# Softmax row sums: matmuls read both key halves of the exponentials, and VectorE's addition of the halves is left out

## The reference

```python
x = x * s1[:, None, :]
x = (x - mu) * jax.lax.rsqrt(var + EPS_IN)
q = heads(jnp.einsum('bsh,oh->bso', x, q_weight) * q_dc[:, None, :])
k = heads(jnp.einsum('bsh,oh->bso', x, k_weight) * k_dc[:, None, :])
v = heads(v_flat)
attn = jnp.einsum('bhqd,bhkd->bhqk', q, k) * scale
attn = jax.nn.softmax(attn, axis=-1)
out = jnp.einsum('bhqk,bhkd->bhqd', attn, v).transpose(0, 2, 1, 3).reshape(B, S, H)
out = jnp.einsum('bsh,oh->bso', out, w_weight) * w_dc[:, None, :]
```

## Time and profile before

| what | value |
|---|---|
| timed runs, median (lowest to highest) | 718.82 us (718.27 to 719.84) |
| profiled execution, span from the first to the last instruction | 718.9 us |
| mean granted TensorE clock, share of full speed | 0.903 |
| attention stage in the profiled execution | about 0 to 300 us |
| TensorE busy | 515.4 us, 72% |
| VectorE busy | 500.2 us, 70% |
| ScalarE busy | 263.7 us, 37% |

### The profile page before, as it was taken

One profiled execution on the slowest core, in us unless ns is written; L12 is line 12 of the kernel. 1 busy time (PEld: TensorE's weight loads), 2 busy tenths in 40 slices (PEclk: granted clock), 3 DMA queues, 4 the chain that ended last, 5 costly groups with the idle time before them and its releaser, 6 DMA issues.

```text
span 718.9 us, 10868 instructions
## 1 busy us (share of the span) xinstructions
PE 515.4 (72%) x3248; PEld 302.7 (42%) x3264; DVE 500.2 (70%) x820; ACT 263.7 (37%) x513; POOL 129.9 (18%) x136
## 2 busy tenths in 40 slices
PE   3667888888888878999972100187677668888878
PEld 2555556465564634688862000011111113333357
DVE  2834858667595775467666897188898878888832
ACT  2314453445545433366673555012112112222211
POOL 5302012020120200240000246011221112222100
PEclk9868999999999998999995555589999989999999
DMA  9635161624606240040000234644454446556341
GB/s 356 216 71 103 31 129 26 113 52 80 118 16 130 51 81 1 1 175 0 0 0 1 88 117 157 77 90 86 98 98 93 92 85 128 117 115 135 84 147 51
DMA packets 44889, 64.88 MB, mean 90 GB/s; under 512 B 19536, under 2 KB 34256, under 8 KB 41152
## 3 DMA queue, kind: packets, MB, share of 16 engines
q1 hardware_dynamic: 41520, 59.26, 37.0%
q0 software_dynamic: 784, 3.15, 1.1%
q10 hardware_dynamic: 2560, 2.16, 0.9%
HBM read 41.88 MB, written 22.61 MB: 90 GB/s over the span
## 4 chain that ended last, share of the span: by engine, by line
PE 37%; issue 20%; DVE 19%; DMA 10%; ACT 7%; POOL 4%; SPq 2%; ACTq 0%; DVEq 0%; POOLq 0%
DVE zst L1378 15%; PE bank L718 6%; PE bank L965 6%; ACT ex L540 5%; PE bank L975 5%; PE bank L736 4%; DMA bst<-bd_d 3%; DMA qst<-mT 3%; PE bank L746 3%; PE bank L1061 2%; PE bank L773 2%; PE bank L727 2%; PE bank L756 2%; POOL xpart L416 2%; DVE mx L1175 2%
## 5 line engine op out<-in xcount | busy, mean ns | idle before, releaser
L1378 DVE CUSTOM_DVE_ANT_0 zst<-zst,bank,hi 128x512 f32<-128x512 f32 x256 | 191.3, 747 | 43.6 <-PE bank L965 22.2
L965 PE MATMUL bank<-xst,bst 128*128 128x512 bf16 x240 | 87.5, 404 | 102.5 <-DMA bst<-bd_d 57.7
L648 ACT ACTIVATE yb<-bank,ybias 128x512 f32<-128x512 f32 x64 | 44.1, 689 | 186.9 <-PE bank L975 182.4
L965 PEld LDWEIGHTS bank<-xst,bst 128*128 128x128 bf16 x256 | 24.7, 98 | 187.3 <-DVE zst L1378 120.5
L1175 DVE TENSOR_REDUCE mx<-bank 128x2 f32<-128x512 f32 x128 | 80.0, 686 | 18.1 <-PE bank L736 17.0
L540 ACT ACTIVATE ex<-bank 128x512 f32<-128x512 f32 x128 | 66.1, 609 | 41.1 <-PE bank L746 23.5
L975 PE MATMUL bank<-zst,cst 128*32 128x512 f32 x512 | 70.2, 621 | 0.9 <-DVE zst L1378 0.9
L1193 DVE TENSOR_TENSOR esum<-ex 128x1024 f32<-128x1024 f32 x32 | 39.1, 1223 | 42.7 <-ACT ex L540 42.7
L1237 DVE SCALAR_TENSOR_TENSOR acc<-xrp,wcv,acc 128x256 f32<-128x256 f32 x96 | 40.1, 481 | 29.4 <-ACT acc L580 28.8
L877 PE MATMUL bank<-xres,win 128*128 (+1 forms) x256 | 57.6, 382 | 1.2 <-ACT gateT L585 0.7
L718 PE MATMUL bank<-xnT,w 128*128 128x256 f32 x192 | 52.3, 422 | 5.1 <-ACT xnT L487 5.1
(11 more groups left out here) (169 smaller groups left out, 712.3 us busy)
## 6 DMA issues: line engine op xcount, KB each, us to landing
qk_d<-part SPq DMA_DIRECT2D x64, 96.0 KB, 2.5
xs_d<-xpart SPq DMA_DIRECT2D x16, 384.0 KB, 2.6
xst<-xs_d SPq DMA_DIRECT2D x32, 192.0 KB
xst<-xs_d SPq DMA_DIRECT2D x32, 128.0 KB
y_d<-yb SPq DMA_DIRECT2D x128, 32.0 KB
ytk<-y_d SPq DMA_DIRECT2D x16, 256.0 KB, 3.6
bst<-bd_d SPq DMA_DIRECT2D x32, 102.0 KB
qst<-qk_d SPq DMA_DIRECT2D x8, 384.0 KB, 4.6
```

The lines of the kernel that those rows point to most:

```text
L648: nc.scalar.activation(yb[:, par, g, :], bank[4 + n % 2][:, :], ACT.Identity, bias=ybias[:, bass.ds(i * (2 * CH // 4) + n, 1)]).then_inc(s ...
L965: mm(bank[k][:, :], bst[:, par, step, :], xst[:, par, step, :], start=True, stop=True)\
L1378: v._custom_dve(bass.dve_ops.TENSOR_ADD_SAT, out=zst[:, t % ZR, :], in0=zst[:, (t - 1) % ZR, :], in1=bank[t % 4][:, :], s0=hi[:, t:t + 1], ...
```

## The change

The tensor esum, its semaphore es_ready and VectorE's add_tiles are taken out. The sums matmuls read ex directly, once for each key half, and accumulate in PSUM: eight matmuls in a group where there were four. pv_done is set by the last of them.

```diff
-        esum = sb0("esum", [P, 2, 4, S])
...
                 if sums:
-                    pe.wait_ge(s["es_ready"], b * 4 + (g + 1))
-                    for r in range(4):
-                        ins = mm(bank[2 * o + 1][32 * r:32 * r + 32, 0:S], half_ones[:, par, :], esum[:, g % 2, r, :],
-                                 start=par == 0, stop=par == 1, skip_group_check=True)
+                    for t in range(HALVES):
+                        for r in range(4):
+                            ins = mm(bank[2 * o + 1][32 * r:32 * r + 32, 0:S], half_ones[:, par, :],
+                                     ex[:, g % 2, r, t * S:(t + 1) * S], start=par == 0 and t == 0,
+                                     stop=par == 1 and t == HALVES - 1, skip_group_check=True)
                     ins.then_inc(s["pv_done"], 1)
                     return
...
-                def add_tiles(g):
-                    dve.wait_ge(s["exp_done"], b * NH + (4 * g + 4))
-                    if not (first and g < 2):
-                        dve.wait_ge(s["pv_done"], b * 4 + (g - 1))
-                    v.tensor_tensor(esum[:, g % 2, :, :], ex[:, g % 2, :, 0:S], ex[:, g % 2, :, S:], ALU.add)\
-                        .then_inc(s["es_ready"], 1)
-
...
-                add_tiles(0)
-                add_tiles(1)
                 if more:
                     normalise(b + 2, False)
-                add_tiles(2)
                 attend(0)
-                add_tiles(3)
                 if not last:
                     dve.wait_ge(s["mt_done"], b + 1)
                     maxima(b + 1, 0, EARLY)
```

More of the change, by code:

```diff
@@ L218, in build @@
             cast1 part_ready pw ld_q0 ld_q1 ld_k0 ld_k1 m_row smax_done maxes mt_done mT_ready st_done exp_done
-            es_ready pv_done att_ready wu_done x1_ready wcomp wgain pconst xr_done xr_in tap3_ready gate_done
+            pv_done att_ready wu_done x1_ready wcomp wgain pconst xr_done xr_in tap3_ready gate_done
             gate_out conv_done xcT_ready xcT_used raw_ready tok_ready tok_taken xn_ready sq_done part0 part1 rem0
```

## The result

| | median us | lowest to highest | runs |
|---|---|---|---|
| before | 719.33 | 718.27 to 720.86 | 4 |
| changed | 727.29 | 726.17 to 730.94 | 4 |

The ratio is 1.0135, 95% interval 1.0092 to 1.0178: the changed kernel is slower by 8 us by the medians and by 9.7 us by the ratio (0.0135 x 719). All medians in this document are over every execution, while the ratios leave out three slow ones: 720.24 us of e8, 1704.4 us of e9, and 774.79 us of the kernel before beside e9 to e11.

What follows compares the result with a forecast made beforehand. The prediction took a chain of waits, not a busy engine, to bound the kernel. Six seams 7.7, the seventh 0.9 and the last sample 0.8 us gave +9.4, so 718.8 became 728.2 us, range 725.0 to 731.0.

Steps and rivals of the forecast that it cites:

- The unit, 0.43 us: Attention sums on TensorE: each group doubled from four to eight matmuls takes 0.43 us longer, 1.07 against 0.64.
- Rival 1: Sums matmuls: weight loads of added rounds not hidden, each exposed group costs 0.64 us, total 732.8 us; chance 0.04.
- Three of four groups exposed in six seams: Ends of samples 0 to 5: sums groups 0, 1 and 3 each add 0.43 us, 1.29 a seam, 7.7 in all.
- Rival 2: Six seams: group 3 hidden because transposes already wait for something else, 2.6 us less, 725.6 us; chance 0.09.
- The seventh seam, +0.86: Seam without transposes: last sums end before the maxima, so only groups 0 and 1 count, +0.86 us.
- 1.5 us either way: Seventh seam: TensorE's clock drop may fall earlier or later, or miss L773, changing the time by up to 1.5 us.
- The last sample, +0.78: Last sample: exponentials 0.86 us later, sums directly behind L763 end at 292.90 against 292.12, +0.78 us.
- rival 3: Sums doubling free in TensorE's idle time; only the last sample changes, -0.5 us, 718.3 us; chance 0.05.
- buys less than 0.1 us: Last sample: removing both adds on the chain gains under 0.1 us, as the exponentials were only just ahead.
- rival 4: Seams: VectorE is the hidden bound, so removing the adds makes the kernel faster, -1.7 us, 717.1 us; chance 0.04.
- The sum: Whole kernel: six seams 7.7, seventh seam 0.9 and last sample 0.8 us give +9.4 us.
- the same for this purpose: Whole kernel before: profiled span 718.9 us and median of timed runs 718.82 us taken as equal.

Runs made afterwards that it cites:

- e8: Changed kernel, sums of groups 0 and 1 directly behind their weighting, next sample's transposes ahead of group 3's sums: 714.5 us, ratio 0.9948.
- e9: Kernel before, additions kept, with only the next sample's transposes moved ahead of the sums of group 3: 720.41 us, ratio 1.0014.
- e11: Repeat of e8, the changed kernel with sums directly behind their weighting and transposes first: 715.33 us, ratio 0.9952.
- e3: Changed kernel with eight sums matmuls for groups 0 and 1, four for groups 2 and 3: 723.86 us, ratio 1.0059.
- e4: Changed kernel with eight sums matmuls for group 3 alone, four for the others: 722.53 us, ratio 1.0037.
- e5: Changed kernel with eight sums matmuls for group 2 alone, four for the others: 718.58 us, ratio 0.9985.
- e2: Changed kernel with four sums matmuls in every group, no additions, second key half left out: 717.44 us, ratio 0.9979.
- e1: Kernel before with VectorE's additions kept and the sums matmuls doubled, both rounds reading esum: 727.85 us, ratio 1.0114.
- e7: Changed kernel with the sums of groups 0 and 1 moved ahead of the next scores, directly behind their weighting: 717.58 us, ratio 0.998.

## Why the prediction was right

**The unit, 0.43 us.** Right: 1.04 against 0.61 us on the chain, 512 records with a mean of 383 ns. The nearest row, L763, had given the price exactly. Rival 1, open weight loads, is out: 16 loads of 32 columns take 0.59 us beside 1.07 us of matmuls in the timeline of the changed kernel, and the group is 0.43 us longer, not 0.64. The rule of the Trainium skill ("TensorE: Matmul & The Clock Gate", Part 3) that loads overlap matmuls in flight only with another row group doesn't describe these column strips, where all loads have all 128 rows; the measurement decides.

**Three of four groups exposed in six seams.** Right: 1.25 to 1.28 us a period against 1.29 forecast, and e3, e4 and e5 give 0.83, 0.40 and 0. Rival 2 is out by e4.

**The seventh seam, +0.86.** The mechanism was right and a part of it came back. From the second set of scores (249.35 before, 254.44 after) to the score behind attT (268.04 and 273.99) it takes 18.69 us before and 19.55 after, exactly 0.86 more. From there to the transposes of the maxima it takes 8.47 us and then 7.97: TensorE's clock fell later. Before, the granted clock is 0.50 from 268 us to 274 us. The windows of the changed kernel answer to the earlier trace rows:

```profile
271.00:274.00 3.00, 0.41 (x4) 0.13 (x4) 2.96 (x5) 0.00 (x0) 0.00 (x0) 1.00 0.00 0
274.00:277.00 3.00, 2.18 (x11) 0.60 (x12) 3.00 (x6) 0.00 (x0) 0.00 (x0) 0.86 0.00 0
277.00:280.00 3.00, 3.00 (x10) 2.44 (x11) 2.31 (x4) 0.00 (x0) 0.00 (x0) 0.57 0.00 0
```

The idle stretch is the same 2.39 us, but behind it the clock holds longer and comes near the level of 1.2 GHz (0.57 over 277 to 280 us) only at L773. The prediction had this as 1.5 us either way; it was 0.5 us in favour.

**The last sample, +0.78.** Measured 281.96 to 298.36, 16.40 us, against 15.61: +0.79.

**The additions are worth 0.5 us.** That is what the prediction's sum has for them in the last sample, 0.43 + 0.86 - 0.78 = 0.51, and what rival 3 has; its sentence that taking them out "buys less than 0.1 us" doesn't agree with that sum and is wrong. By e2 it is 0.52 us, and by e1, whose last sample takes 16.8 us where the changed kernel takes 16.4, about 0.4. Rival 3 (the doubling is free) is out by e1, and rival 4 (VectorE is the bound) by e2.

**Where a step was off.** The sum was 9.4 us, and the two profiled executions differ by 5.5 us. The end of the last sums was forecast near 301.5 and came at 298.36, 6.2 us later than before. The 3.2 us that are missing have names: the first transposes of maxima, ahead of any changed work, came 1.00 us earlier (60.14 against 61.14); the projection behind the first second-set scores ran 0.4 us shorter, with the clock still rising (L727 3.55 us, L726 3.13); the long DMA in the second period of before, 1.1 us; and the clock in the seventh seam, 0.5 us. These are 3.0 us. Behind 310 us the distance between the two executions shrinks by another 0.7 us, which is not explained here. The first two lie in work that the change leaves as it was. The last comes with the later start of the stage, and whether the long DMA has to do with the length of the seams is open, since it came in four profiles of kernels with short seams and in none of the changed kernel. The step that was off is that the span of the profiled execution and the median are "the same for this purpose": in the runs of the changed kernel the time is 1.8 us over the span (726.17 and 724.4), so the profiled execution of before stood 1.4 to 1.9 us above its median. The forecast starts from the median and isn't touched by it, but a comparison of the two spans is. The median over several executions, +8.0, +7.6 and, with the additions kept, +8.9 us, is the better measure of the sum, and it is 0.5 to 1.8 us below it. The pieces as measured give 6 x 1.26 + 0.86 - 0.5 + 0.79 = 8.7 us.

**The loads.** "The loads of the next sample's qst and kst only gain slack" holds for the change, whose longer seams leave TensorE no wait for kst between 80 and 235 us. How little slack there was, e7 shows: there the last weighting comes 0.84 us sooner behind the second set of scores than before (11.02 against 11.86 us), and the loads end the wait.

## What to carry to other kernels

Before an operation goes from one engine to another, look where the receiving engine's copy of it stands, not how busy the engine is: 0.43 us of matmuls cost nothing ahead of a wait and their full length between a score and the exponential that waits for the buffer. If the removed work was what fixed the order, use the freedom at once; the same instructions in another order were 9 us faster than the change as made. And expect the next limit close behind: here a load and the reciprocal's place in VectorE's queue each stood within a microsecond of the seam, so that gains of 3 to 4 us on paper came to 0 to 3.

## What the runs showed of the hardware

Four fp32 matmuls of 32 columns, with 256 moving columns each and in four column strips, add 0.43 us together as a further round, also when the stationary is the same in all of them. That is what one fp32 matmul of 128 columns takes (L718: four matmuls, eight records, 1.73 us on the chain). The weight loads of such a round, 106 to 111 ns each, are nowhere on the path. The DMA of one row of maxima took 1.78 to 3.62 us in one execution, on a path that passes it eight times, which is more than some of the differences looked for here.
